# Expert weights issued by SyncE and prepared in a planned setup step; b2 added by VectorE instead of a TensorE product

## The reference

```python
def ffn(x):                                   # E = 8 experts, top 2, hidden 256
    logits = einsum('bsd,ed->bse', x, gate_w) + gate_b
    probs = softmax(logits); topk_vals, topk_idx = top_k(probs, 2)
    h = relu(einsum('bsd,edh->bseh', x, w1) + b1)
    expert_out = einsum('bseh,eho->bseo', h, w2) + b2
    return sum of the two chosen expert_out, weighted by topk_vals
def attn(x):                                  # 8 heads of 32, latent rank 64
    q = x @ Wq.T; kv = x @ Wkv_down.T; k = kv @ Wk_up.T; v = kv @ Wv_up.T
    return softmax(q k^T / sqrt(32)) v @ Wo.T
x = x + 0.5 * ffn(layernorm(x))
x = x + attn(layernorm(x))
x = x + 0.5 * ffn(layernorm(x))
```

## Time and profile before

| | |
|---|---|
| median of 3 runs | 1355.59 us |
| the profiled execution | 1360.36 us |
| its span | 1358.6 us |
| TensorE busy | 90% |
| VectorE busy | 61% |
| GpSimd busy | 59% |
| ScalarE busy | 52% |
| 16 DMA engines, mean over the span | 150 GB/s |
| TensorE's granted clock, mean | 0.948 |

### The profile page before, as it was taken

One profiled execution on the slowest core, in us unless ns is written; L12 is line 12 of the kernel. 1 busy time (PEld: TensorE's weight loads), 2 busy tenths in 40 slices (PEclk: granted clock), 3 DMA queues, 4 the chain that ended last, 5 costly groups with the idle time before them and its releaser, 6 DMA issues.

```text
span 1358.6 us, 26424 instructions
## 1 busy us (share of the span) xinstructions
PE 1216.4 (90%) x8853; PEld 804.5 (59%) x8853; DVE 822.4 (61%) x2234; ACT 712.1 (52%) x1469; POOL 795.4 (59%) x783
## 2 busy tenths in 40 slices
PE   2888889999979989989989899999999988989893
PEld 1575466666655555556756565656565655657573
DVE  2745747686577655676638766764677836455242
ACT  1334556656645555656565456666555555545430
POOL 1012674765556757765385667768757675657633
PEclk9877999898989899989999899999998999989997
DMA  9204564762645165425645353544464327657741
GB/s 310 109 8 125 175 192 125 238 188 67 182 147 163 34 194 178 119 82 151 202 144 156 90 171 96 181 132 143 138 180 132 111 64 226 204 172 226 222 152 50
DMA packets 167913, 203.12 MB, mean 150 GB/s; under 512 B 17050, under 2 KB 112482, under 8 KB 167780
## 3 DMA queue, kind: packets, MB, share of 16 engines
q1 hardware_dynamic: 146944, 166.36, 39.9%
q0 software_dynamic: 15360, 31.49, 7.9%
q10 hardware_dynamic: 5476, 3.59, 0.8%
HBM read 153.53 MB, written 47.84 MB: 148 GB/s over the span
## 4 chain that ended last, share of the span: by engine, by line
PE 48%; POOL 15%; DVE 12%; issue 9%; DMA 9%; ACT 4%; ACTq 1%; SPq 1%; POOLq 0%; DVEq 0%
PE psum L1455 42%; POOL pairs L955 7%; POOL Y L1006 5%; DMA Y<-results_C,posC 4%; POOL slots_C L986 3%; DVE neg_m L1410 3%; DVE X L1394 3%; PE psum L1676 3%; DMA slots_C<-xnC,posC 2%; DMA Y<-results_A,posA 2%; ACT probs L1093 2%; PE psum L1554 1%; PE psum L1619 1%; PE psum L1518 1%; DVE ntC L1262 1%
## 5 line engine op out<-in xcount | busy, mean ns | idle before, releaser
L1410 DVE TENSOR_REDUCE neg_m<-psum 128x1 f32<-128x512 f32 x512 | 317.0, 682 | 175.2 <-PE psum L1455 137.6
L955 POOL TENSOR_TENSOR pairs<-probs 128x512 f32<-128x512 f32 x256 | 321.0, 1277 | 64.6 <-ACT probs L1093 61.1
L1455 PE MATMUL psum<-nat 32*128 32x512 f32 x2048 | 349.3, 641 | 7.0 <-DVE neg_m L1410 3.0
L1093 ACT ACTIVATE probs<-psum 128x512 f32<-128x512 f32 x512 | 264.6, 607 | 94.5 <-PE psum L1455 78.1
L986 POOL DMA_INDIRECT slots_A<-xnA,posA x120 | 117.2, 976 | 194.2 <-DVE posA L1378 84.7
L1455 PEld LDWEIGHTS psum<-nat 32*128 32x128 f32 x2048 | 137.4, 186 | 113.8 <-issue 38.3
L1455 PEld LDWEIGHTS psum<-xg_T,wt 128*128 128x128 f32 x1296 | 161.0, 198 | 40.3 <-issue 20.0
L1006 POOL DMA_INDIRECT Y<-results_C,posC x120 | 116.3, 969 | 114.0 <-DMA Y<-results_C,posC 74.3
L1455 PE MATMUL psum<-xg_T,wt 128*128 128x128 f32 x1296 | 177.9, 287 | 2.6 <-DMA wt<-packed 1.1
L986 POOL DMA_INDIRECT slots_C<-xnC,posC x120 | 118.5, 987 | 92.0 <-DMA slots_C<-xnC,posC 55.5
L1006 POOL DMA_INDIRECT Y<-results_A,posA x120 | 116.0, 967 | 87.2 <-DMA Y<-results_A,posA 51.0
(11 more groups left out here) (191 smaller groups left out, 1602.5 us busy)
## 6 DMA issues: line engine op xcount, KB each, us to landing
wt<-packed SPq DMA_DIRECT2D x324, 320.0 KB
xs<-slots_A SPq DMA_DIRECT2D x36, 256.0 KB
results_A<-ys SPq DMA_DIRECT2D x36, 256.0 KB
xs<-slots_C SPq DMA_DIRECT2D x36, 256.0 KB
results_C<-ys SPq DMA_DIRECT2D x36, 256.0 KB
X<-in_L_attn_x_dram SPq DMA_DIRECT2D x16, 256.0 KB, 5.3
out_dram<-X SPq DMA_DIRECT2D x16, 256.0 KB
packed<-probs SPq DMA_DIRECT2D x1, 2560.0 KB, 7.8
```

What stands on the lines that cost most here:

```text
L955: pool.tensor_tensor(pairs[:, kt // 2, j, :], probs[:, kt - 1, j, :], probs[:, kt, j, :], ALU.add).then_inc(S["p_added"], 1)
L1093: act.activation(probs[:, kt, j, :], at.banks()[j][:], ACT.Exp, scale=SCALE).then_inc(a_done, 1)
L1410: V_.tensor_reduce(neg_m[:, g, n, j:j + 1], at.banks()[j][:], AX.X, ALU.max, negate=True).then_inc(d_done, 1)
L1455: return nc.tensor.matmul(dst, w, m, start=start, stop=stop)
```

## The change

- SyncE issues the attention and expert weights right behind X of batch 0, as a planned step (weights), ahead of the other 15 batches' X. ScalarE issues only the gate's two transfers.
- b1 and b2 come as one row each. sum_experts becomes ten products of 512 columns: two spread b2 over all partitions, eight (four pairs) give w1's column sums minus b1. ScalarE makes the high parts and copies b2 into the pack; VectorE subtracts.
- turn_attention, sum_experts and their counterparts on ScalarE and VectorE form a planned step (setup) before the first top1, and after the first logits. The gate's second product comes behind the first xTf.
- b2 stands in all 128 partitions of a packed expert. The product with b2_rows in y is gone; VectorE adds b2 from wt where it empties y's bank, so y moves from ring "a" to ring "d", and the place of a quad's weights and its bank are freed by VectorE. In dy the b2 product has one row instead of 128, with the same columns.
- The zero fill of the slots goes in pieces of 992 values instead of 128; that of C comes behind the pack.
- All numbers of the wanted-time table differ, so the order differs all over.

```diff
-PERIOD, FIRST_B = 37.1, 69.39
+PERIOD, FIRST_B = 38.24, 31.97
...
-    "y": ((("PE", 2.1), ("ACT", 0.48)), 0.0), "ystore": ((("SP", 0.48),), 4.2),
+    "y": ((("PE", 1.75), ("DVE", 0.65)), 0.0), "ystore": ((("SP", 0.48),), 4.2),
...
+    "weights": ((("SP", 6.5),), 6.0), "setup": ((("PE", 4.0), ("ACT", 2.5), ("DVE", 6.0)), 0.0),
...
-D_STEPS = ("xT", "logits", "rank1", "rank2", "wo", "sum", "max", "dy")
-A_STEPS = ("q", "k", "v", "s", "pv", "mrow", "h", "y", "xg", "xTf", "dh")
+D_STEPS = ("xT", "logits", "rank1", "rank2", "wo", "sum", "max", "dy", "y")
+A_STEPS = ("q", "k", "v", "s", "pv", "mrow", "h", "xg", "xTf", "dh")
...
+    wanted["A", 0, "load", 0], wanted["A", 0, "weights", 0], wanted["A", 0, "setup", 0] = -1000.0, -999.0, -998.0
...
-                steps[s, c, "y", q].gives.append((0, "w"))
+                steps[s, c, "y", q].gives.append((1, "w"))
...
-    after(("A", 0, "pack", 0), ("A", 0, "top1", 0))
+    after(("A", 0, "weights", 0), ("A", 0, "load", 0), part=0)
+    after(("A", 0, "setup", 0), ("A", 0, "weights", 0), ("A", 0, "logits", 0))
+    for key in (("A", 0, "pack", 0), ("A", 0, "dh", 0), ("B", 0, "q", 0), ("A", 0, "top1", 0)):
+        after(key, ("A", 0, "setup", 0))
+    first_part(("A", 0, "blank", 0), ("A", 0, "weights", 0))
+    first_part(("A", 0, "blank", 1), ("A", 0, "pack", 0))
...
-        b1_all = [Y[:, i, :, :, :].rearrange("p k n d -> p (k n d)").rearrange("p (e h) -> p e h", e=EXPERTS // 2)
-                  for i in range(2)]
+        b1_row = Y[0:1, :, :, :, :].rearrange("p i k n d -> p (i k n d)")
...
+            def weights(at):
+                for dst, src in (
+                    (wq_raw, wq.rearrange("(g p) d -> p g d", p=P)), (wo_raw, wo),
+                    (wk_raw, wk_up.rearrange("(g p) r -> p g r", p=P)),
+                    (wv_raw, wv_up.rearrange("(g p) r -> p g r", p=P)),
+                    (down_raw, wkv_down),
+                ):
+                    sp.dma_start(dst, src).then_inc(weights_in, 16)
+                sp.dma_start(pack[:, :, 0:HID], w1.rearrange("e p h -> p e h")).then_inc(experts_in, 16)
+                sp.dma_start(b1_row[:, 0:EXPERTS * HID], b1.rearrange("e h -> (e h)").unsqueeze(0)).then_inc(experts_in, 16)
+                sp.dma_start(b2_row[:, 0:EXPERTS * D], b2.rearrange("e d -> (e d)").unsqueeze(0)).then_inc(experts_in, 16)
+                for u in range(UNITS):
+                    sp.dma_start(pack[:, :, W2C + u * D:W2C + (u + 1) * D], w2[:, u * P:(u + 1) * P, :].rearrange("e p d -> p e d")
+                                 ).then_inc(experts_in, 16)
...
-                    sp.wait_ge(a_full, counts["a_full", (s0, c0, "y", q0)])
+                    sp.wait_ge(d_done, counts["d_done", (s0, c0, "y", q0)])
...
             act.dma_start(gw_raw, gate_w).then_inc(gate_in, 16)
-            act.dma_start(gate_bias[:], gate_b.partition_broadcast(P)).then_inc(gate_in, 16)
-            act.dma_start(pack[:, :, 0:HID], w1.rearrange("e p h -> p e h")).then_inc(experts_in, 16)
-            for e in range(EXPERTS):
-                act.dma_start(b1_all[e // 4][:, e % 4, :], b1[e].partition_broadcast(P)).then_inc(experts_in, 16)
-            for u in range(UNITS):
-                act.dma_start(pack[:, :, W2C + u * D:W2C + (u + 1) * D], w2[:, u * P:(u + 1) * P, :].rearrange("e p d -> p e d")
-                              ).then_inc(experts_in, 16)
-            for row in (0, B2_LOW):
-                act.dma_start(b2_raw[row:row + 1, 0:EXPERTS * D], b2.rearrange("e d -> (e d)").unsqueeze(0)).then_inc(experts_in, 16)
-            for dst, src in (
-                (wq_raw, wq.rearrange("(g p) d -> p g d", p=P)), (wo_raw, wo),
-                (wk_raw, wk_up.rearrange("(g p) r -> p g r", p=P)),
-                (wv_raw, wv_up.rearrange("(g p) r -> p g r", p=P)),
-                (down_raw, wkv_down),
-            ):
-                act.dma_start(dst, src).then_inc(weights_in, 16)
+            act.dma_start(gate_bias[:], gate_b.partition_broadcast(P)).then_inc(gate_bias_in, 16)
             act.preload_act_table_set("natural_log_exp_and_others")
...
+            def setup(at):
+                act.wait_ge(setup_pe, 3)
+                act.activation(up_T, psum[5][0:RANK, :], ACT.Copy).then_inc(setup_act, 1)
+                act.activation(wqkv_h[:, 0, :], psum[7][:, 0:HD], ACT.Copy).then_inc(setup_act, 1)
+                act.activation(wo_T[:].rearrange("p g d -> p (g d)"), psum[7][:, HD:HD + GROUPS * D], ACT.Copy).then_inc(setup_act, 1)
+                act.wait_ge(setup_pe, 4)
+                act.activation(wqkv_h[:, 1:3, :].rearrange("p a n -> p (a n)"), psum[4][:], ACT.Copy).then_inc(setup_act, 1)
+                for i in range(2):
+                    act.wait_ge(setup_pe, 5 + i)
+                    act.activation(pack[:, 4 * i:4 * i + 4, B2C:WCOLS], psum[5 + i][:].rearrange("p (e d) -> p e d", e=4), ACT.Copy).then_inc(setup_act, 1)
...
-            def split_attention():
...
-            def split_experts():
+            def setup(at):
+                dve.wait_ge(consts_made, 1)
+                dve.wait_ge(setup_act, 3)
+                V_.tensor_tensor(wqkv_l[:, 0, :], psum[7][:, 0:HD], wqkv_h[:, 0, :].bitcast(F32), ALU.subtract).then_inc(setup_dve, 1)
+                dve.wait_ge(setup_act, 4)
+                V_.tensor_tensor(wqkv_l[:, 1:3, :].rearrange("p a n -> p (a n)"), psum[4][:],
+                                 wqkv_h[:, 1:3, :].rearrange("p a n -> p (a n)").bitcast(F32), ALU.subtract).then_inc(setup_dve, 1)
                 dve.wait_ge(experts_in, 16 * EXPERT_DMAS)
                 for i in range(4):
-                    fix = b1_all[i // 2][:, i % 2 * 2:i % 2 * 2 + 2, :]
                     own = pack[:, 2 * i:2 * i + 2, 0:HID]
-                    dve.wait_ge(setup_pe, 5 + i)
-                    chain(V_.tensor_tensor(fix, fix, psum[i][:].rearrange("p (e h) -> p e h", e=2), ALU.subtract))
-                    V_.scalar_tensor_tensor(out=own, in0=fix, scalar=1.0 / D, in1=own, op0=ALU.mult, op1=ALU.add).then_inc(setup_dve, 1)
-                V_.tensor_copy(pack[0:1, :, B2C:WCOLS].bitcast(F32R),
-                               b2_raw[0:1, 0:EXPERTS * D].rearrange("p (e d) -> p e d", e=EXPERTS))
-                for i in range(2):
-                    part = slice(i * EXPERTS // 2, (i + 1) * EXPERTS // 2)
-                    low = slice(B2_LOW, B2_LOW + 1)
-                    high_b2 = b2_high[low, 0:EXPERTS // 2 * D]
-                    raw = b2_raw[low, i * EXPERTS // 2 * D:(i + 1) * EXPERTS // 2 * D]
-                    chain(V_.tensor_copy(high_b2.bitcast(F32R), raw))
-                    last = V_.tensor_tensor(pack[low, part, B2C:WCOLS].bitcast(F32R), raw.rearrange("p (e d) -> p e d", e=EXPERTS // 2),
-                                            high_b2.rearrange("p (e d) -> p e d", e=EXPERTS // 2), ALU.subtract)
-                    if i == 0:
-                        chain(last)
-                last.then_inc(pack_done, 1)
...
+            def y(at):
+                i = at.turn(quad_turn)
+                bank = ring(at)
+                tiles = quad_tiles(at.index, at.k)
+                first, _ = w_place(at.stage, at.index, tiles[0])
+                if i >= YS_RING:
+                    dve.wait_ge(y_out[i % YS_RING], ring_count(i - YS_RING, YS_RING))
+                V_.tensor_tensor(ys[:, i % YS_RING, 0:len(tiles), :], bank[:, 0:len(tiles) * P].rearrange("p (i d) -> p i d", d=D),
+                                 wt[:, first:first + len(tiles), B2C:WCOLS], ALU.add).then_inc(d_done, 1)
...
             def sum_experts():
                 pe.wait_ge(experts_in, 16 * EXPERT_DMAS)
+                pe.wait_ge(setup_dve, 2)
+                for i in range(2):
+                    pe_mm(psum[5 + i][:], ones[0:1, :], b2_row[:, 4 * i * D:4 * (i + 1) * D]).then_inc(setup_pe, 1)
                 for i in range(4):
-                    pe_mm(psum[i][:].rearrange("p (e h) -> p e h", e=2), ones[:], pack[:, 2 * i:2 * i + 2, 0:HID]).then_inc(setup_pe, 1)
+                    pe_mm(psum[i][:].rearrange("p (e h) -> p e h", e=2), ones[:], pack[:, 2 * i:2 * i + 2, 0:HID], stop=False)
+                    pe_mm(psum[i][:], minus_one[:], b1_row[:, 2 * i * HID:2 * (i + 1) * HID], start=False).then_inc(setup_pe, 1)
                 pe.wait_ge(setup_dve, 8)
-                pe.wait_ge(pack_done, 1)
+                pe.wait_ge(setup_act, 6)
+                pe.wait_ge(consts_made, 1)
+            def setup(at):
+                before = order["PE"][:order["PE"].index(at.step)]
+                pe.wait_ge(a_done, max(counts["a_full", step] for step in before if step[2] in A_STEPS))
+                pe.wait_ge(d_done, max(counts["d_full", step] for step in before if step[2] in D_STEPS))
+                turn_attention()
+                sum_experts()
...
-                first, _ = w_place(s, c, tiles[0])
-                pe_mm(bank[:, 0:len(tiles) * D].rearrange("p (i d) -> p i d", d=D), b2_rows[:],
```

(13 more changed lines are left out.)

139 lines of the change are left out of this document (57 added, 82 removed).

## The result

| | before | after |
|---|---|---|
| median (lowest to highest) | 1355.4 us (1354.8 to 1357.0) | 1369.4 us (1365.4 to 1378.7) |
| profiled execution, its span | 1360.4, 1358.6 us | 1371.8, 1370.0 us |

A forecast was written before the change was run, and what follows sets the result against it. TensorE was taken to lead 68% of the middle, GpSimd the rest; start and end were separate regimes. -13.8 - 17.9 + 1 - 4.6 = -35.3 us gave 1325 us profiled, 1320 us as median, own range 1309 to 1331.

The forecast's parts named there:

- The dense chunk's b2 products keep their columns: 0.: Dense chunks: their b2 products, keeping their columns, were priced at no change, 0 us.
- Head, -13.8: Start: first dense expert product at 28.8 instead of 44.58 us, less 2 us for queued work; bounds -5 and -19.
- Three slow and 17 at 0.45 give 10.2 us: Start: time of the ten setup products, two records each, with fast spacing after three slow records.
- the 2 us for batch 1: Start: 2 us allowed because ScalarE's norm and scaling of batch 1 precede the copy the setup's second product needs.
- The 3 us that I left to the range: Start: TensorE would enter the dense chunk at full clock, about 3 us better, not counted in the sum.
- Rival C: Start: SyncE stuck issuing, weights land near 26 us, head gives only 5 us: 1329 us, chance 0.05.
- The b2 product in y, -17.9: Middle: removing 84 products saves 27.6 us, 26.3 counting, times 0.68; bounds 0 and -26.3.
- my 0.68: Middle: share of the time between 100 and 1282 us that TensorE leads, 800 of 1182 us.
- y on VectorE, +1: Middle: 56 us of y's work moves to VectorE and ScalarE loses 49.1; net +1 us, low bound -4.
- Tail, -4.6: End: 14 gather pairs instead of 15 behind GpSimd's last addition, 4.6 us each; bounds 0 and -5.
- Rival D: Middle: VectorE releases y late, so TensorE waits for weights; 0.6 us per quad gives +50, 1370 us; chance 0.08.
- B: Middle: GpSimd binds it, so only head and tail arrive, 18.4 us: 1337 us, chance 0.17.

The follow-up runs named there:

- a_both: Changed kernel with the dense chunks' b2 product on 128 rows and the one-row column-sum products issued first: 1342.2 us, ratio 0.9931; on another chip 1340.2 us.
- a_b2r: a_both with b2 put into y's banks by an fp32r TensorE product again, VectorE only copying: 1352.4 us, ratio 1.0002, 12.2 us above a_both on the same chip.
- b_nob2: Kernel before without the product that puts the experts' b2 into y's banks, same step order: 1351.0 us, ratio 0.9995.
- a_yq: a_both with VectorE emptying and adding b2 to only the first 128 of each y bank's 512 columns: 1336.5 us, ratio 0.9865.

## Why the prediction was wrong

**"The dense chunk's b2 products keep their columns: 0."** This step failed, and it alone turned the sign. The columns stayed and the rows fell from 128 to one. The runs show 19 us for it in the kernel before and 24 us in the changed one: 12.5 us in each dense chunk, the second of which took the end over from the gathers. I counted columns, and none of my numbered rows shows this product.

**Head, -13.8.** The mechanism was right, the size was not: the first dense product came 3.3 us sooner, not 13.8. "Three slow and 17 at 0.45 give 10.2 us": the ten products took 19.8 us (20.73 to 40.5). Twenty records at 0.87 us are 17.4 us; the 2.4 us above that are the changes of rows, and the other 7.2 of the 9.6 us are the slow record spacing, which I took to end after three records, as it did before with 128-row products alone, and which one-row products did not leave. Ordering the products gave back 4.1 us of both (a_both). The start of the sums, forecast at 19.8 with the 2 us for batch 1, was off by 0.9. The 3 us that I left to the range for a dense chunk entered at full clock did not come in the change; with the sums in order they did (3.70 us for eight records against 6.33). Rival C's sign, later than 38 us, came true without its cause: it had the weights land near 26 us, and the first sum of w1 began at 24.4.

**The b2 product in y, -17.9.** Mis-sized: 12.2 us by a_b2r. The array's time was too large: some 18 us by y's own rows for all 84 products, not 27.6. The share of it that shows, 12.2 of 18, is near my 0.68, but in an order made for it; by the engines' sums, 13 to 15 us, it would be near 0.9. The low bound of 0 is what b_nob2 gave in the old order.

**y on VectorE, +1.** Too small if anything; a_yq allows 4 to 9, which is not settled. The middle gained 7.5 us instead of 16.9, which these two terms can make up within the 5 us by which executions of a kernel differ (a_both's two profiles have middles of 1185.4 and 1190.8 us).

**Tail, -4.6.** The step was right and its price too high: from the last addition to the issue of the last gather 14 pairs took 65 us, 15 had taken 67, so a pair less gave 2 us and not 4.6. What was late next was named (TensorE, 14 us to spare) and not priced: 12.5 us of dense chunk and 9 us more work behind the last addition used it up. "Products of TensorE behind B15's last scores are about as many as before" does not hold for those behind the last addition, 403 records against 341. With 128 rows the tail is 1.2 us shorter than before.

**Rival D** gave 1370 us and came within 1 us of the median, for a reason that isn't there: a_both keeps VectorE's release and the change's order and stands near 1341. Its sign came close, for TensorE waited 9.9 us for packed weights in 14 places (before 2.7 in 3; D's mark was 10), but a_both still waits 7.6 us. B's sign did not show: between 400 and 1100 us the matmuls of line 1454 alone are 48% of the chain. A rival's number that fits doesn't make its mechanism right. The forecast of 1320 was out of reach even without the two row mistakes, by some 20 us.

## What to carry to other kernels

Price a TensorE product by its columns and by what stands beside it: each change of the number of rows in use (1 or 32 against 128) costs 0.2 us here, so give a small product zeros up to the others' 128 rows, or put products of few rows in a row. Look at a product's cost with and without it, not only at the distance to the next start. And in a planned kernel hold the order fixed when a term is tested; a table of numbers made for other steps cost 51 to 64 us.

## What the hardware showed that I had not expected

A product of one row is dearer than one of 128: 1.06 us against 0.67 us for a group of three in which only one differs, and 32 rows are as dear as one. One-row products of 512 columns (two records each) ran with 0.87 us a record after TensorE had just been at a clock of 0.92, and the clock fell to 0.50 while they ran back to back; TensorE's rows show no idle time there. It came back with 128-row products. In a_both's busy time by stretch the granted clock reads 1.00 while its records have the same 0.87 us:

```profile
25.00:30.00 5.00, 5.00 (x7) 1.99 (x6) 0.00 (x0) 0.44 (x3) 0.00 (x0) 1.00 0.23 85
```

So at the start of an execution the spacing of like records tells the clock better than the column does.
